# Opening and ending of a one-core matmul kernel in Strassen form: tokens loaded in a new layout, a bias row split for TensorE, other orders, the last result in parts

## The reference, cut to what matters

```python
x: (64, 128, 1024)   cond: (64, 512)   W3: (512, 1024)   W2: (1024, 1024)
q_emb = relu(cond @ W3 + b3)                       # (64, 1024)
v_sum = sum(x, axis=1)                             # over the 128 tokens of a sample
y = (128 * x + v_sum) * q_emb[:, None, :]
out = x + relu(y @ W2 + b2)
```

## Time and profile before

| what | value |
|---|---|
| median of 3 runs | 636.22 us |
| the profiled execution's own time | 635.75 us |
| its span, first to last instruction | 634.0 us |
| outside the span | 1.75 us |
| TensorE busy | 629.2 us, 99% |
| VectorE busy | 444.1 us, 70% |
| ScalarE busy | 418.9 us, 66% |
| GpSimd busy | 16.5 us, 3% |
| mean granted TensorE clock | 1.000 |
| mean DMA rate | 172 GB/s |

### The profile page before, as it was taken

One profiled execution on the slowest core, in us unless ns is written; L12 is line 12 of the kernel. 1 busy time (PEld: TensorE's weight loads), 2 busy tenths in 40 slices (PEclk: granted clock), 3 DMA queues, 4 the chain that ended last, 5 costly groups with the idle time before them and its releaser, 6 DMA issues.

```text
span 634.0 us, 9260 instructions
## 1 busy us (share of the span) xinstructions
PE 629.2 (99%) x2795; PEld 518.4 (82%) x2796; DVE 444.1 (70%) x675; ACT 418.9 (66%) x897; POOL 16.5 (3%) x21
## 2 busy tenths in 40 slices
PE   9999999999999999999999999999999999999997
PEld 6888888888888888888888888888888888888886
DVE  3989979576776757677576776757677576776533
ACT  4879886839577594856839577494866839577320
POOL 2340000000000000000000000000000000000000
PEclk9999999999999999999999999999999999999999
DMA  8935736454353734436353353733346353350703
GB/s 301 400 138 196 264 136 227 173 197 143 141 182 132 256 141 135 137 158 232 132 199 137 139 187 132 255 142 131 134 165 232 132 199 132 144 189 0 259 6 132
DMA packets 26656, 108.83 MB, mean 172 GB/s; under 512 B 2961, under 2 KB 3089, under 8 KB 22802
## 3 DMA queue, kind: packets, MB, share of 16 engines
q1 hardware_dynamic: 26496, 108.54, 47.9%
q10 hardware_dynamic: 146, 0.14, 0.1%
HBM read 75.11 MB, written 33.55 MB: 171 GB/s over the span
## 4 chain that ended last, share of the span: by engine, by line
PE 92%; DVE 2%; issue 0%; POOL 0%; ACT 0%; DVEq 0%
PE acc L285 92%; DVE vsum L597 1%; DVE w_lo L678 1%; DVE scale L603 0%; DVE a_lo L662 0%; POOL x_sb L572 0%; DVE xn L686 0%; ACT a_hi L386 0%; DVE bias L605 0%; DVEq L691 0%
## 5 line engine op out<-in xcount | busy, mean ns | idle before, releaser
L285 PE MATMUL acc<-w_hi,a_hi 128*128 128x512 f32 x904 | 352.2, 390 | 0.2
L285 PE MATMUL acc<-w_lo,a_hi 128*128 128x512 f32 x904 | 351.7, 389 | 0.0
L285 PE MATMUL acc<-w_hi,a_lo 128*128 128x512 f32 x904 | 351.7, 389 | 0.0
L404 ACT ACTIVATE x_sb<-x_sb,bias,scale 128x128 f32<-128x128 f32 x492 | 203.2, 486 | 9.6 <-DVE bias L605 9.5
L285 PEld LDWEIGHTS acc<-w_hi,a_hi 128*128 128x128 f32 x904 | 169.7, 188 | 36.7 <-DVE a_lo L662 1.0
L285 PEld LDWEIGHTS acc<-w_hi,a_lo 128*128 128x128 f32 x904 | 169.7, 188 | 35.4
L285 PEld LDWEIGHTS acc<-w_lo,a_hi 128*128 128x128 f32 x904 | 169.7, 188 | 35.0
L673 DVE TENSOR_TENSOR a_lo<-x_sb,a_hi 128x512 fp32r<-128x512 f32 x150 | 103.5, 690 | 106.9 <-ACT a_hi L399 106.2
L399 ACT CAST a_hi<-x_sb 128x512 fp32r<-128x512 f32 x150 | 93.3, 622 | 39.5 <-PE acc L285 38.1
L399 ACT CAST a_hi<-s 128x512 fp32r<-128x512 f32 x60 | 37.4, 623 | 74.0 <-PE acc L285 69.1
L597 DVE TENSOR_REDUCE vsum<-x_sb 128x16 f32<-128x2048 f32 (+1 forms) x38 | 73.7, 1943 | 6.9 <-DMA x_sb<-x_t 6.7
(11 more groups left out here) (49 smaller groups left out, 192.9 us busy)
## 6 DMA issues: line engine op xcount, KB each, us to landing
xn<-x SPq DMA_DIRECT2D x64, 512.0 KB, 4.0
out<-xn SPq DMA_DIRECT2D x62, 512.0 KB, 3.2
x_sb<-x_t SPq DMA_DIRECT2D x30, 1024.0 KB, 5.1
x_sb<-w_t SPq DMA_DIRECT2D x4, 512.0 KB, 6.1
x_sb<-x_t SPq DMA_DIRECT2D x8, 256.0 KB, 11.7
u_sb<-w_q SPq DMA_DIRECT2D x3, 512.0 KB, 8.0
m_sb<-w_q SPq DMA_DIRECT2D x3, 512.0 KB, 7.6
w_stage<-w_q SPq DMA_DIRECT2D x2, 512.0 KB, 9.0
```

Source lines behind the costliest of these rows:

```text
L285: return nc.tensor.matmul(dst, lhs, rhs, start=False, stop=False, skip_group_check=True)
L404: last = nc.scalar.activation(x_sb[:, slot, t, k], x_sb[:, slot, t, k], ACT.Identity, bias=bias[:, slot, t, k:k + 1], scale=scale[:, slot, ...
```

## The change

The tokens' layout in DRAM and SBUF has the K half outside the sample, so that two quarters (both samples of one half) are one contiguous run, and the first pair is loaded in four DMAs of 512 KB in place of eight of 256 KB. b11's first half is loaded in two parts. The row of b2 is split into a high and a low fp32r part (ScalarE and VectorE), and seeds banks 3, 2 and 4 by matmuls, in place of the warming matmuls, the float32 row and two ScalarE seeds. q_sum(6) and q_sum(7) stand ahead of tile 1 of product 0, and their q_relu ahead of the casts of b11's pieces 2 and 3. Quarter 7 is scaled on VectorE; `b_step` is made there too. The last result is made in four parts, stored by SyncE and ScalarE by turns. The diff, cut to its core (expressions that only follow the new layout are left out):

```diff
-    SEEDED = (2, 4, 5, 6, 7, 0, 1)
+    ROWS = (3, 2, 4)
+    SEEDED = (5, 6, 7, 0, 1)
...
-        x_sb = sb("x_sb", [P, 4, TWO, KT, N])
+        x_sb = sb("x_sb", [P, 4, 2, TWO, KH, N])
...
+        row_hi = a_hi[0:1, 6].rearrange("p k n -> p (k n)")
+        row_lo = a_lo[0:1, 6].rearrange("p k n -> p (k n)")
+        row_ones = a_hi[0:1, 3, 0]
...
 SyncE, loads
             def load_first(n):
-                (t, h), c, _ = MADE[n]
-                sp.dma_start(quarter(c, (t, h)), x_t[c, :, t, h * KH:(h + 1) * KH]).then_inc(x0_loaded[n], 16)
+                (_, h), c, _ = MADE[2 * n]
+                sp.dma_start(x_sb[:, c, h], x_t[c, :, h]).then_inc(x0_loaded[n], 16)
...
+            def load_b11(k):
+                sp.dma_start(w_stage[:, k], w2_q[0, 0, :, k * MH:(k + 1) * MH]).then_inc(b11_first[k], 16)
...
             load_first(0)
+            load_w3(2)
+            load_b11(0)
+            load_w3(3)
+            load_b11(1)
+            load_half(w_halves, 0, 0, 1, b11_loaded)
             load_first(1)
-            load_w3(2)
-            load_half(w_halves, 0, 0, 0, b11_loaded)
-            load_w3(3)
-            load_half(w_halves, 0, 0, 1, b11_loaded)
             load_first(2)
             load_b(b_first, 0, b_first_loaded)
-            for n in (3, 4):
-                load_first(n)
             for h in range(2):
                 load_half(u_halves, 1, 0, h, b21_loaded)
-            for n in (5, 6, 7):
-                load_first(n)
+            load_first(3)
...
 SyncE, end
+            for n in (0, 2):
+                part = slice(n * MH // 4, (n + 1) * MH // 4)
+                sp.wait_ge(part_done, n + 1)
+                sp.dma_start(out[2 * (2 * p + 1) + 1, :, part], xn[:, 1, 1, part]).then_inc(tail_stored, 16)
...
 TensorE
             for k in range(KT - 2):
                 q_sum(k)
-                if k == KH - 1:
-                    pe.wait_ge(ones_set, 1)
-                    pe.wait_ge(row_loaded, 16)
-                    add(acc[:, 3], ones[:], b_row)
-                last = keep_warm(1)
-            last.then_inc(marked, 1)
+                if k == 1:
+                    pe.wait_ge(row_hi_ready, 1)
+                    b_row_part(0, row_hi)
+                if k == 2:
+                    pe.wait_ge(row_lo_ready, 1)
+                    b_row_part(0, row_lo)
+                if k == 3:
+                    b_row_part(1, row_hi)
+                if k == 4:
+                    b_row_part(1, row_lo)
+                    b_row_part(2, row_hi)
+            b_row_part(2, row_lo).then_inc(marked, 1)
...
-                    if n == 0 and k == KH // 2:
+                    if n == 0 and k == 1:
                         q_sum(KT - 2)
                         q_sum(KT - 1)
+                    if n == 0 and k == KH // 2:
                         pe.wait_ge(lo_ready, 1)
...
 ScalarE
+            act.wait_ge(ones_set, 1)
+            nc.scalar.copy(row_ones, ones[:])
+            act.wait_ge(row_loaded, 16)
+            nc.scalar.copy(row_hi, b_row).then_inc(row_hi_ready, 1)
             act.wait_ge(small_loaded, 16)
             for k in range(KH):
                 q_relu(k)
             cast_first_half(0)
-            cast_w("b11", 0, b11_loaded[0], 16)
+            cast_w("b11", 0, b11_first[0], 16)
             cast_first_half(1)
-            cast_w("b11", 1, b11_loaded[0], 16)
             for k in (4, 5):
                 q_relu(k)
-            for k in range(2, W_PIECES):
-                cast_w("b11", k, b11_loaded[k // 2], 16)
-            cast_first(1)
+            cast_w("b11", 1, b11_first[1], 16)
             for k in (6, 7):
                 q_relu(k)
-            act.wait_ge(marked, 1)
-            act.wait_ge(b_first_loaded, 16)
-            seed_plain(2, b_first)
+            for k in range(2, W_PIECES):
+                cast_w("b11", k, b11_loaded[1], 16)
+            cast_first(1)
             scale_first(2)
             cast_first(2)
             act.wait_ge(q_ready, KT)
-            for bank in (4, 5):
-                seed_plain(bank, b_first)
+            act.wait_ge(marked, 1)
+            act.wait_ge(b_first_loaded, 16)
+            seed_plain(5, b_first)
...
+                    if first and i in (3, 4):
+                        seed_r(p, i - 3)
-                    if i in (5, 6):
+                    if i in (5, 6) and not first:
...
+            for n in (1, 3):
+                part = slice(n * MH // 4, (n + 1) * MH // 4)
+                act.wait_ge(part_done, n + 1)
+                act.dma_start(out[B - 1, :, part], xn[:, 1, 1, part]).then_inc(last_stored, 16)
...
 GpSimd
-            for n in (1, 4, 7):
+            for n in (1, 4):
                 scale_first(n)
...
-            pool.wait_ge(b_seeded, len(SEEDED))
-            nc.gpsimd.tensor_tensor(b_step[:], b_step[:], b_first[:], ALU.subtract).then_inc(b_step_ready, 1)
...
 VectorE
+            dve.wait_ge(row_hi_ready, 1)
+            nc.vector.tensor_tensor(row_lo, b_row, row_hi.bitcast(fp32), ALU.subtract).then_inc(row_lo_ready, 1)
             sums_0(0)
...
-            for k in range(1, W_PIECES):
-                low_w("b11", k)
+            low_w("b11", 1)
+            low_w("b11", 2)
             sums_0(2)
             scalars_0(2)
+            low_w("b11", 3)
             low_first(1)
             sums_0(3)
             scalars_0(3)
+            scale_first(3)
+            low_first(2)
             sums_0(4)
-            low_first(2)
             scalars_0(4)
-            scale_first(3)
+            low_first(3)
+            low_w("b21", 0)
             sums_0(5)
             scalars_0(5)
-            low_first(3)
-            low_w("b21", 0)
...
             scalars_0(7)
+            scale_first(7)
+            low_first(6)
...
-            for h in range(2):
-                low_w("b22", h)
+            dve.wait_ge(b_seeded, len(SEEDED))
+            nc.vector.tensor_tensor(b_step[:], b_step[:], b_first[:], ALU.subtract).then_inc(b_step_ready, 1)
+            low_w("b22", 0)
             low_first(8)
+            low_w("b22", 1)
...
-            for c in range(2):
-                c21(p, 1, c)
+            c21(p, 1, 0)
+            dve.wait_ge(prod_done, done_by(p, 4, 1))
+            for n in range(4):
+                part = slice(n * MH // 4, (n + 1) * MH // 4)
+                o = xn[:, 1, 1, part]
+                nc.vector.scalar_tensor_tensor(o, p_bank(1, 1)[:, part], 0.0, o, ALU.max, ALU.add).then_inc(part_done, 1)
```

More of the change, by code:

```diff
@@ L10, in cond_residual @@
     AX = mybir.AxisListType
-    UNITS, P, TWO, KT, N = x_t.shape
+    UNITS, P, _, TWO, KH, N = x_t.shape
     PAIRS = UNITS // 2
@@ L18, in cond_residual @@
     B = UNITS * TWO
-    KH = KT // 2
+    KT = 2 * KH
     D = KT * P
@@ L271, in _ @@
                 sp.dma_start(out[2 * (2 * p + c)], xn[:, c, 0]).then_inc(stored[c][0], 16)
-            for r, h in ((c22_done, 1), (c21_done, 0)):
-                half = slice(h * MH, (h + 1) * MH)
-                for c in range(2):
-                    sp.wait_ge(r, 2 * p + c + 1)
-                    sp.dma_start(out[2 * (2 * p + c) + 1, :, half], xn[:, c, 1, half]).then_inc(tail_stored, 16)
+            for c in range(2):
+                sp.wait_ge(c22_done, 2 * p + c + 1)
+                sp.dma_start(out[2 * (2 * p + c) + 1, :, MH:], xn[:, c, 1, MH:]).then_inc(tail_stored, 16)
+            sp.wait_ge(c21_done, 2 * p + 1)
+            sp.dma_start(out[2 * (2 * p) + 1, :, :MH], xn[:, 0, 1, :MH]).then_inc(tail_stored, 16)
+            for n in (0, 2):
+                part = slice(n * MH // 4, (n + 1) * MH // 4)
+                sp.wait_ge(part_done, n + 1)
+                sp.dma_start(out[2 * (2 * p + 1) + 1, :, part], xn[:, 1, 1, part]).then_inc(tail_stored, 16)
             for c in range(2):
@@ L279, in _ @@
                 sp.wait_ge(stored[c][1], 16 * (PAIRS - 1))
-            sp.wait_ge(tail_stored, 64)
+            sp.wait_ge(tail_stored, 80)
+            sp.wait_ge(last_stored, 32)
         @block.tensor
@@ L294, in q_sum, with b_row_part @@
                 last.then_inc(q_summed, 1)
[L296 to L299, removed]
+            def b_row_part(n, part):
+                return add(acc[:, ROWS[n]], row_ones, part)
             pe.wait_ge(warm_set, 1)
@@ L304, in _ @@
                 nc.tensor.matmul(acc[:, n], warm[:, :P], warm[:], start=True, stop=True)
-            keep_warm(4)
+            for _ in range(4):
+                add(acc[:, 2], warm[:, :P], warm[:])
             pe.wait_ge(small_loaded, 16)
@@ L402, in scale_quarter @@
                 t, h = q
-                for k in range(h * KH, (h + 1) * KH):
-                    last = nc.scalar.activation(x_sb[:, slot, t, k], x_sb[:, slot, t, k], ACT.Identity,
-                                                bias=bias[:, slot, t, k:k + 1], scale=scale[:, slot, t, k:k + 1])
+                for k in range(KH):
+                    last = nc.scalar.activation(x_sb[:, slot, h, t, k], x_sb[:, slot, h, t, k], ACT.Identity,
```

(38 more changed lines are left out.)

40 lines of the change are left out of this document (23 added, 17 removed).

## The result

The kernel after takes 642.21 us (median of 5 runs, 641.98 to 644.74) against 636.18 before (5 runs, 635.31 to 636.4): a ratio of 1.0105, 95% interval 1.0085 to 1.0125. It is slower by 6.0 us, where 636.8 with a range to 638.2 was forecast.

The account below looks back on a forecast made before the run. TensorE was taken to bound the kernel, its matmuls unbroken from 45.63 us, so only the opening and end could move. Head +0.75 and end -0.15 gave +0.6 us, a median of 636.8 us, range for all cases 634.9 to 638.2.

Parts of the forecast that it names:

- part 1: Opening up to product 0: shorter TensorE list and earlier data start product 0 at 12.63 us, 0.46 earlier.
- rival B: Opening: the thinner matmul stream lets TensorE's clock fall, costing 1.7 us, to 638.5 us; chance 0.07.
- part 2: Product 0: moved q_sums and q_relus delay casts; tiles 2 and 3 wait 1.07 and 0.6 us, product 1 starts at 19.12.
- Rival A: Product 0: ScalarE's order doesn't bite, pieces 2 and 3 are ready when due; 635.1 us, chance 0.13.
- Part 3: Rest of the opening: the 0.4 us wait ahead of product 11 goes; it starts at 46.4; head +0.75 us.
- Part 4: The end: last result in four parts with smaller stores, -0.15 us, bounds -0.5 and +0.4.
- Rival C: Opening: b2's row lands late or operand 2's 0.5 us margin is eaten; about +1, 637.8 us, chance 0.11.

Follow-up runs that it names:

- Experiment 4: before_one_row_warm: the kernel before with its six warming matmuls in the stretch of q_sums on one partition in place of 128; 641.9 us, ratio 1.0094.
- experiment 5: full_rows: the kernel after with its six row parts on all 128 partitions, operands cleared first; 637.28 us, ratio 1.0019.
- relu_back: The kernel after with q_relu(6) and q_relu(7) back behind the casts of b11's pieces 2 and 3; 641.7 us, ratio 1.009.
- experiment 2: The kernel before with five of its six warming matmuls in the stretch of q_sums left out; 636.67 us, ratio 1.0009.
- warm_back: The kernel after with one 128-row warming matmul put back behind each of q_sum(0) to q_sum(5), row parts kept; 640.91 us.
- before_order: The kernel before with q_sum(6), q_sum(7) ahead of tile 1 and their q_relus ahead of the casts of pieces 2 and 3; 637.18 us, ratio 1.0021.
- experiments 6 and 8: 6: the kernel after with row parts on 128 partitions and q_relu(6), q_relu(7) behind the casts of pieces 2 and 3, 635.13 us; 8: before_order, 637.18 us.
- experiment 7: The kernel before with only the last result in four parts, stored by turns from SyncE and ScalarE; 636.2 us, ratio 1.0007.

## Why the prediction was wrong

**What failed: two assumptions of part 1, and the price and chance of rival B.** Part 1 took a row part for a warming matmul in another place: 0.23 us, 1.07 with a q_sum, and the sum had nothing for the clock. Its nearest row was the float32 row of b2 with the warming matmul behind it, 1.37 together, and that row already says that a one-row matmul isn't cheap; I booked it as a saving and didn't ask what a one-row matmul costs beside one of 128 rows. Measured: 0.43, and 1.46 with the q_sum behind it.

Rival B had the right mechanism, the granted clock falling in the thinner opening, with a chance of 0.07 and a price of 1.7 us, from a stretch as long as the start's. The argument against it, that q_sums with few wide matmuls kept the clock up from 5.43 to 13.09, looked at how many wide matmuls there are and at their columns, and not at their rows. The change has as many (six for six), but on one partition. Experiment 4 makes that edit alone in the kernel before and loses 6.0 us; experiment 5 takes it back in the kernel after and gains 4.7. The stretch at half speed was 13.7 us, not 3.4. How it came to be so long is read from the traces, not tested: at the low clock the one-row list runs on to 15.7, and behind tile 0 product 0 then has its two q_sums, at 1.6 each there. The clock was back 8.7 us behind the start of product 0. In experiment 4, where two tiles stand ahead of the q_sums, it was back after 4.4 (16.82 to 21.2). The waits of part 2 aren't needed for it: relu_back has none, and its clock was back 9.0 us behind product 0. In experiment 2 the fall is over after 3.4 us and costs 0.8, which is nearer to the price I gave.

The loss by terms, against my own times: product 0 started at 15.74 in place of 12.63 (3.1: 0.9 for the three one-row parts at the full clock, 5.26 us from the first q_sum to q_sum(4) in place of 4.37; 2.5 from there on, the low clock with three more of them in it; less 0.3 of an earlier start), and lasted 9.08 in place of 6.49 (2.6, the clock). 3.1 + 2.6 = 5.7 behind my forecast for product 1; the whole was 5.4 behind the forecast for the median.

The Trainium skill, TensorE: Matmul & The Clock Gate, section on oscillation, ties the fall to waits between groups of matmuls. In the kernel of that section they are waits of 3 to 5 us for a DMA. Here the clock fell with the engine busy 2.00 of 2.00 us and no such wait ahead of it, only the 0.25 us ahead of a weight load, so the page names the danger and not its condition in this case; the measurement decides.

**What held.** Part 2, the order on ScalarE: two waits of 1.1 and 0.6 were worked out from the lists and rows. They are in the profile of full_rows at 17.01 and 18.31 to within 0.1 us, in warm_back, and, as 1.2 us of time, in before_order. Rival A (the order doesn't bite) falls by experiments 6 and 8. Part 3 held too: no wait ahead of product 11 is left. The forecast was for a clock that stays up, and full_rows, with the same row parts but for their partitions, took 637.28 (636.17 to 637.73), near 636.8. Part of that match is luck: full_rows is 1.3 us over the kernel before run beside it, where +0.6 was forecast, and its profiled execution, one of its two fastest, began its q_sums at 5.26, not at 5.43. From there product 0 is 7.35 us off, 7.20 by part 1. Part 4, -0.15 us, is not distinguishable from zero in experiment 7, and 3.20 against 3.25 us in the traces. A store of 64 KB landed 1.7 to 1.8 us behind its issue, one of 256 KB 2.0; I had 0.45 less. The Trainium skill's fit in DMA: Bandwidth & Descriptors, section on the anatomy of one DMA, would have it 0.45 less as well, but it is a fit for DMAs that GpSimd issues, and these came from SyncE and ScalarE; 0.2 to 0.3 was measured. Rival C didn't show: b2's row was there at 5.2 us, since its cast on ScalarE began at 5.16, and no wait for operand 2 stands in the chain of full_rows, which names TensorE alone from 18.31 on.

**Open.** The runs don't tell whether one row as such doesn't count for the clock, or whether it is the slower stream that one-row matmuls make: in experiments 4 and 5 both change together. warm_back has the kernel before's six warming matmuls of 128 rows and the one-row parts besides, and two of its four executions lost the clock; why only two isn't settled. Whether the load order and the larger loads bring anything by themselves wasn't tried alone. Product 0's 0.5 us earlier start at the full clock (12.61 against 13.09) holds 0.17 of an earlier first q_sum; the other 0.3 is what they and the shorter list bring together.

## What to carry to other kernels

A warming matmul can't be swapped for a useful one by counting matmuls and columns: look at how many partitions the useful one uses, and read the granted clock in short stretches of the opening, since a busy share of 99% hides a halved clock. If a one-row operand must go through TensorE in a thin stretch, clear the other partitions and use all 128 rows; here that cost three small memsets and gained 4.7 us. On an engine that works in order, an operation moved ahead costs what it waits for, and that can be worked out to a tenth of a microsecond from the timelines.

## What the runs showed of the hardware that was not expected

- A matmul of one partition takes longer than one of 128: fp32r, 512 columns, 0.43 us to the next start against 0.31 on 128 partitions in the same place (7.04 to 7.47 in the kernel after, 6.96 to 7.27 in full_rows); bf16, 0.31 against 0.22. The q_sum behind it is longer too, 1.03 against 0.81 us.
- The granted clock fell from 1.00 to 0.50 with TensorE busy 2.00 of 2.00 us by the profile and no wait for a semaphore ahead of it, in the kernel after and in before_one_row_warm.
- When TensorE gets fast at the start differs from one execution to the next: the first q_sum began at 5.10 in a profile of 634.24 us and at 5.58 in one of 634.76 us of the same kernel, and at up to 6.29 in others (relu_back). This may be much of the 1.3 us over which the runs of before are spread (635.41 to 636.72); only one execution of before was profiled, so it isn't shown. The clock column doesn't tell it: it reads 1.00 from the start, though the first warming matmuls of the kernel before start 0.43 us apart (1.60 to 2.03), and those behind 4.57 about 0.22.
